# Nine groups of up to seven pairs a tile for fourteen of four, and turned blocks in the sums' banks

## The chip, the cores and the metric

The kernel runs on one core of a Trainium2 chip. The metric is the device time of one execution, in microseconds. Of the kernel before there are three runs, with a median of 2292.99 us (2291.53 to 2293.34), and one profiled execution.

## The reference

A graph with N = 12,500 nodes of H = 64 features and E = 400,000 edges; `src` and `dst` are drawn at random and sorted by `dst`. After a layer norm and a ReLU, two rounds of message passing with a GRU cell follow, and the input is added at the end:

```python
    for t in range(num_rounds):
        src = x[row]
        dest = x[col]
        m_input = jnp.concatenate([dest, src, edge_attr], axis=1)
        messages = m_input @ msg_W[t].T + msg_b[t]
        agg = jax.ops.segment_sum(messages, row, num_segments=x.shape[0])
        x = _gru_cell(agg, x, gru_Wih[t], gru_bih[t], gru_Whh[t], gru_bhh[t])
    return x
  ...
  h = jnp.maximum(_layernorm(x, axis=-1), 0.0)
  x = x + _L0_gnn_ref(h, edge_index, edge_weight1, ...)
```

Here `row` is `src` and `col` is `dst`. The message weights are linear, so the kernel sums the features of the `dest` nodes of each node's edges first, and the weights come in afterwards, in the gates. Each round is therefore a gather of 400,000 rows by `dst` and a sum of them by `src`.

## The kernel before, in words

The nodes are cut into 98 tiles of 128 for the sums (by `src`) and into windows for the rows that are gathered (by `dst`), C = 104 of them, each of at most 128 nodes. A sort at the start, up to about 741 us, puts the edges into slots: each pair of a tile and a window has 64 slots. Then come round 1 (about 741 to 1510 us) and round 2 (about 1533 to 2272 us), in which every tile goes through the same steps. Two windows make a pair: a tile has 52 pairs.

- **gather** (PE, L1298). A one-hot matrix for each window, made by DVE from the slots' lanes (`dst1`, named `planes` in the rows), times the window's rows: 2 matmuls of 128 columns for a pair, into a bank of PSUM (`ps_rows`).
- **take** (ACT, L1399). It copies the gathered rows of one unit, a group of pairs, from PSUM to SBUF as fp16.
- **scatter** (PE, L1320 in round 1, L1318 in round 2, whose operands are exchanged). The taken rows times a second one-hot matrix (`src1`, `src` in the rows): 2 matmuls for a pair, which add up in the tile's bank `ps_sum`. There are two such banks, for even and odd tiles.
- **sums** (ACT, L1410 and L1406): copies the sum of a finished tile. **node_sums** (DVE, L1525 to L1535 and L1516, L1520) makes `joined`, `scaled` and, in round 1, `extras` from it.
- **turn** (PE, L1337 to L1340; two matmuls in round 2, L1332 and L1333): transposes these blocks in `ps_T`, a bank of its own; **take_turned** (ACT, L1417) copies them out.
- **gates** (PE, L1353 and L1355), then for each pair of tiles sigmoid `rz` (ACT, L1429, odd tiles), **tanh_inputs** (DVE, L1543, L1545), tanh `cand` (ACT, L1446, even tiles), **mix** (DVE). In round 1 ACT and DVE cut the new features into two fp16 parts: high (ACT, L1435, odd tiles), the rest (**left_over**, DVE, L1561), low (ACT, L1440, even tiles).

The order on every engine is written out by hand in a function `body(s, b, half)`, called for each tile s (b is 0 for even tiles, 1 for odd ones). `in_pairs` (L62) unrolls the first few tiles and puts the others into a hardware loop of two tiles. The 52 pairs are cut into NU = 14 units, ten of 4 pairs and four of 3 (`UJ`, `PAIR_AT`). On PE, unit u of a tile is gathered and then unit u - LAG is scattered, with LAG = 3; the last three units of a tile are scattered beside the first gathers of the next. Where the small steps stand among the units is told by five numbers, `TURN_AT` 1, `SUM_AT` 3, `GATES_AT` 5, `SIGMOID_AT` 8, `TANH_AT` 3. Gathers use four rooms of one bank in turn, and one waits for the take of four units earlier.

The one-hots are made in NQ = 4 parts of a tile (2048, 2048, 1792 and 768 columns; L1499 by planes and L1503 by source). The lanes for a part are fetched by DMA from SP's queue and from POOL's (L675). In round 1 POOL also copies the edge attributes of each part into the rows (`put_attr`, L1165), and the scatter of the part's first unit waits for that. In round 2 the rows are kept in a ring of four units.

Of the kernel before, what the change touches and what calls it, by code (L numbers as in the profile page):

```python
# [22 lines left out]
P = 128  # L23
# [107 lines left out]
def build(nc, x, src, dst, attr, msg_W, msg_b, Wih, bih, Whh, bhh, out):  # L131
# [15 lines left out]
    NU = 2 * -(-J // (2 * UJ))  # L147
    UQ = -(-NU // NQ)
    FULL = J - NU * (UJ - 1)
    PAIR_AT = [u * UJ - max(u - FULL, 0) for u in range(NU + 1)]  # L150
    QUARTER_AT = [PAIR_AT[min(q * UQ, NU)] for q in range(NQ + 1)]
    assert ROUNDS > 1 and P >= C >= NT and C > HELD and 0 < LAST <= EW and (P - C) * EW <= E and E % P == 0 and PAIR_AT[NU] == J and 0 <= FULL <= NU and all(at % 2 == 0 for at in QUARTER_AT) and NU % 2 == 0 and N * P < 1 << 22 and H == 64 and NT % 2 == 0 and NU > (NQ - 1) * UQ and UQ >= LAG and N >= P
# [18 lines left out]
    SUM_AT, TURN_AT, GATES_AT, SIGMOID_AT, TANH_AT = 3, 1, 5, 8, 3  # L171
# [13 lines left out]
    with ExitStack() as ctx:  # L185
# [914 lines left out]
        def sums_round(r, scope):  # L1100
# [23 lines left out]
            ps_rows = [ps(f"ps_rows{b}", [P, 512], scope=scope) for b in range(4)]  # L1124
# [6 lines left out]
            ps_T = ps("ps_T2", [P, 512], scope=scope)  # L1131
# [47 lines left out]
            with nc.Block() as block:  # L1179
# [108 lines left out]
                def _(te):  # L1288
                    def gather(s, u, b):
# [3 lines left out]
                        wait(te, rows_ready, s * NU + u - 3)  # L1293
                        for k, j in enumerate(pairs_of(u)):
                            for half in range(2):
                                c = 2 * j + half
                                if c < C:
                                    last = nc.tensor.matmul(  # L1298
                                        ps_rows[(u + NU * b) % 4][half * SLOTS:(half + 1) * SLOTS, k * 2 * H:(k + 1) * 2 * H],
                                        dst1[q][:, (c - 2 * QUARTER_AT[q]) * SLOTS:(c - 2 * QUARTER_AT[q] + 1) * SLOTS], rows_of[r % 2][:, c, :],  # L1300
                                        start=True, stop=True)
                        last.then_inc(gathered, 1)

                    def scatter(s, u, b):
# [6 lines left out]
                        if u == 0:  # L1311
                            wait(te, joined_ready if flipped else sum_ready, s - 1)
                        for k, j in enumerate(pairs_of(u)):
                            hot = src1[q][:, (j - QUARTER_AT[q]) // 2, :, j % 2]
                            row = rows_of_unit(u, b)[:, k, :]
# [8 lines left out]
                    def turn(k, b):  # L1324
# [5 lines left out]
                        if flipped:  # L1330
                            te.wait_ge(extras_kept, 1)
                            nc.tensor.matmul(ps_T[high, 0:P], copied[b][:], ident[:], start=True, stop=True)  # L1332
                            nc.tensor.matmul(ps_T[low, 0:P], scaled[b][:], ident[:], start=True, stop=True).then_inc(turned, 1)  # L1333
# [3 lines left out]
                        nc.tensor.matmul(ps_T[low, 0:P], joined[b][:], ident[:], start=True, stop=True)  # L1337
                        nc.tensor.matmul(ps_T[high, 0:P], copied[b][:], ident[:], start=True, stop=True)
                        nc.tensor.matmul(ps_T[high, P:2 * P], extras[b][:], ident[:], start=True, stop=True)
                        nc.tensor.matmul(ps_T[low, P:2 * P], scaled[b][:], ident[:], start=True, stop=True).then_inc(turned, 1)  # L1340
# [21 lines left out]
                    def turn_extras():  # L1362
                        for v in range(2):
                            last = nc.tensor.transpose(ps_T[0:NT, v * P:(v + 1) * P], edge_sums[:, :, v], ident[:])  # L1364
                        last.then_inc(extras_turned, 1)

                    def body(s, b, half):
                        later_tile = past(s, 1)
                        for u in range(NU):
                            gather(s, u, b)  # L1370
# [6 lines left out]
                            if past(s, 2) and u == TURN_AT:  # L1377
                                turn(s - 2, b)
# [501 lines left out]
```

## Time and profile before

| | |
|---|---|
| median of three runs | 2292.99 us (2291.53 to 2293.34) |
| the profiled execution | 2290.76 us |
| its span | 2288.8 us |
| PE, PEld busy | 1507.7 (66%), 1405.6 (61%) |
| DVE, ACT busy | 2132.3 (93%), 1894.5 (83%) |
| POOL busy | 743.5 (32%) |
| takes (L1399) | 2744, 1362.3 us, mean 612 ns |
| one-hots by source (L1503) | 784, 801.4 us, mean 1022 ns |
| one-hots by planes (L1499) | 784, 515.8 us, mean 658 ns |
| scatter L1320, L1318 | 10192 each, 555.9 and 542.0 us |
| gather L1298 | 10192 a round, 545.8 and 535.4 us |
| fetch of lanes to its landing | 3.7 to 4.6 us |

The shares are over the whole span, and a third of it is the sort, where PE hardly works. For the rounds they are to be read by stage. Busy times of successive instructions overlap at their tails: from the start of one to the start of the next is less than what one lasts. PEld is the load of a matmul's weights, which runs beside the matmuls before it.

### The profile page before, as it was taken

How to read it: one execution, taken by the hardware profiler on the slowest of the kernel's cores; microseconds unless marked ns; L12 is line 12 of the kernel's file. 1: busy time of each engine (PE TensorE's matmuls, PEld its weight loads, DVE VectorE, ACT ScalarE, POOL GpSimd, SP SyncE). 2: the span in 40 equal slices, each digit the busy share in tenths (PEclk: the TensorE clock that was granted, in tenths of full speed). 3: DMA queues.
4: the chain of work that ended last, by engine and by line, in shares of the span. 5: the costliest groups of instructions: out<-in, count | busy, mean ns of one | idle time of the engine just before them, and what ended most of it. 6: DMA issues, size and time to landing. Idle time of an engine off the chain costs nothing. (4 is left out here: it accounts for less than half of the span.)

```text
span 2288.8 us, 121076 instructions
## 1 busy us (share of the span) xinstructions
PE 1507.7 (66%) x43734; PEld 1405.6 (61%) x43734; DVE 2132.3 (93%) x3394; ACT 1894.5 (83%) x4474; POOL 743.5 (32%) x1245
## 2 busy tenths in 40 slices
PE   0000000000024899999999999958999999999996
PEld 0000000000013899999999999858999999999996
DVE  8999999999967899999999999958999999999996
ACT  4778795664124899999999999958999999999996
POOL 1000000000085666666666666621222222122222
PEclk9999999999999999999999999979999999999998
DMA  6100001210233676666667777636767777777773
GB/s 124 34 0 0 0 0 36 47 23 22 56 91 88 210 228 231 221 233 228 228 233 226 229 229 229 217 124 215 244 240 240 240 240 240 239 241 239 240 241 118
DMA packets 165648, 375.64 MB, mean 164 GB/s; under 512 B 70877, under 2 KB 87427, under 8 KB 165023
## 3 DMA queue, kind: packets, MB, share of 16 engines
q1 hardware_dynamic: 114427, 191.07, 26.9%
q0 software_dynamic: 49456, 181.94, 24.0%
q10 hardware_dynamic: 1708, 1.97, 0.3%
q8 instruction: 24, 0.39, 0.1%
q14 instruction: 33, 0.27, 0.0%
HBM read 358.39 MB, written 16.17 MB: 164 GB/s over the span
## 5 line engine op out<-in xcount | busy, mean ns | idle before, releaser
L1399 ACT ACTIVATE rows<-ps_rows 128x512 f16<-128x512 f32 (+1 forms) x2744 | 1362.3, 612 | 53.3 <-PE ps_rows L1298 42.9
L1503 DVE TENSOR_TENSOR src<-iota_units,src_lane 128x2048 f16<-128x2048 f16 (+2 forms) x784 | 801.4, 1022 | 26.6 <-PE ps_sum L1318 19.2
L1320 PE MATMUL ps_sum<-rows,src 128*64 128x132 f16 x10192 | 555.9, 222 | 9.0 <-issue 1.6
L1298 PE MATMUL ps_rows<-rows_next,planes 128*64 128x128 f16 x10192 | 535.4, 219 | 36.4 <-DVE planes L1499 21.3
L1298 PE MATMUL ps_rows<-rows_now,planes 128*64 128x128 f16 x10192 | 545.8, 219 | 19.7 <-ACT rows L1399 9.2
L1318 PE MATMUL ps_sum<-src,rows 128*64 128x128 f16 x10192 | 542.0, 220 | 4.8 <-ACT rows L1399 1.2
L1499 DVE TENSOR_SCALAR planes<-planes,lane_no 128x2048 f16<-128x2048 f16 (+2 forms) x784 | 515.8, 658 | 8.7 <-DMA planes<-lanes_dram 8.6
L816 PE MATMUL ps_src<-ident,late 104*64 104x104 f32 x98 | 19.9, 380 | 642.0 <-DVE late L1051 623.4
L1298 PEld LDWEIGHTS ps_rows<-rows_now,planes 128*64 128x64 f16 x10192 | 412.2, 110 | 41.1 <-ACT rows L1399 17.9
L1298 PEld LDWEIGHTS ps_rows<-rows_next,planes 128*64 128x64 f16 x10192 | 397.8, 109 | 60.6 <-DVE planes L1499 21.9
L816 PEld LDWEIGHTS ps_src<-ident,late 104*64 104x64 f32 x98 | 13.7, 162 | 648.1 <-DVE late L1051 624.0
L1320 PEld LDWEIGHTS ps_sum<-rows,src 128*64 128x64 f16 x10192 | 396.6, 110 | 18.1 <-ACT rows L1399 16.3
L1318 PEld LDWEIGHTS ps_sum<-src,rows 128*64 128x64 f16 x10192 | 386.2, 109 | 12.9 <-ACT rows L1399 12.5
L675 POOL DMA_DIRECT2D planes<-lanes_dram x392 | 226.5, 578 | 288.1 <-DVE planes L1499 273.7
L1223 POOL COPY copied<-h 128x64 f32 (+1 forms) x196 | 66.5, 340 | 522.0 <-PE ps_T L1333 512.9
L793 POOL DMA_INDIRECT taken<-lower_dram,start_i x22 | 44.9, 2040 | 581.1 <-issue 581.1
L1165 POOL COPY rows<-attr_room 128x32 f16 (+5 forms) x392 | 220.4, 562 | 0.8 <-PE ps_sum L1320 0.4
L324 ACT ACTIVATE taken<-taken 128x3847 bf16<-128x3847 int32 x49 | 171.0, 3490 | 14.6 <-issue 14.5
L1353 PE MATMUL ps_gates<-w_first,turned_now 128*64 128x256 f32 x784 | 122.1, 378 | 3.1 <-ACT turned_now L1417 1.7
L1355 PE MATMUL ps_gates<-w_second,turned_now 128*64 128x256 f32 x784 | 122.5, 379 | 1.1 <-issue 1.1
L1355 PEld LDWEIGHTS ps_gates<-w_second,turned_now 128*64 128x64 f32 x784 | 64.8, 137 | 19.9
L1417 ACT ACTIVATE turned_now<-ps_T 128x256 f32<-128x256 f32 (+1 forms) x196 | 70.7, 361 | 3.4 <-PE ps_T L1340 2.6
(213 smaller groups left out, 2200.3 us busy)
## 6 DMA issues: line engine op xcount, KB each, us to landing
planes<-lanes_dram POOLq DMA_DIRECT2D x196, 512.0 KB, 4.4
planes<-lanes_dram SPq DMA_DIRECT2D x194, 512.0 KB, 4.6
planes<-lanes_dram POOLq DMA_DIRECT2D x98, 448.0 KB, 4.6
planes<-lanes_dram SPq DMA_DIRECT2D x97, 448.0 KB, 4.6
planes<-lanes_dram POOLq DMA_DIRECT2D x98, 192.0 KB, 3.7
planes<-lanes_dram SPq DMA_DIRECT2D x97, 192.0 KB, 3.9
rows_now<-parts_dram SPq DMA_DIRECT2D x104, 32.0 KB, 1.7
rows_next<-parts_dram SPq DMA_DIRECT2D x104, 32.0 KB, 3.5
```

What stands on the lines that cost most here:

```text
L324: nc.scalar.activation(beyond[:], src_i[:], ACT.Sign, bias=below[:, m:m + 1], accum_out=balance[:, m:m + 1]).then_inc(counts_ready, 1)
L675: plain(engine.dma_start(lanes[q], lanes_dram[bass.ds(s, 1), slots_of_quarter(q)] .broadcast_to([P, n_slots(q)]))).then_inc(lanes_in_of[r] ...
L1165: plain(nc.gpsimd.tensor_copy(rows[:, at, 2 * H:2 * H + 2], attr_two[:, bass.ds(s, 1), at, :] .rearrange("p o j v -> p (o j) v"))).then_in ...
L1298: last = nc.tensor.matmul(ps_rows[(u + NU * b) % 4][half * SLOTS:(half + 1) * SLOTS, k * 2 * H:(k + 1) * 2 * H], dst1[q][:, (c - 2 * QUART ...
L1318: last = nc.tensor.matmul(ps_sum[b][at, 0:P], row[:, at], hot, start=(j == 0), stop=(j == J - 1))
L1320: last = nc.tensor.matmul(ps_sum[b][at, 0:width], hot[:, at], row, start=(j == 0), stop=(j == J - 1))
L1353: nc.tensor.matmul(ps_gates[at, to], turned_now[b][:, at], w_first[:, r, :], start=True, stop=False)
L1355: last = nc.tensor.matmul(ps_gates[at, to], turned_now[b][:, P + at.start:P + at.stop], w_second[:, r, :], start=False, stop=True)
L1399: nc.scalar.activation(rows_of_unit(u, b)[:, :, 0:2 * H], cut(ps_rows[(u + NU * b) % 4][:])[:, 0:n, :], ACT.Copy).then_inc(rows_ready, 1)
L1417: nc.scalar.activation(turned_now[b][:, 0:n], ps_T[:, 0:n], ACT.Copy).then_inc(T_ready, 1)
L1499: nc.vector.tensor_scalar(dst1[q], lanes[q], lane_no[:, 0:1], None, ALU.is_equal).then_inc(dst1_ready, 1)
L1503: nc.vector.tensor_tensor(src1[q][:], iota_units[:].rearrange("p (o l) k -> p o l k", o=1) .broadcast_to([P, pairs_now, P, 2]), src_lane[: ...
```

## The change

The unit is no longer of a fixed size. A tile has three parts, each with units of (7, 7, 4), (7, 7, 4) and (6, 6, 4) pairs: nine units. `ps_rows` has three rooms, of two, two and one bank (8, 8 and 4 pairs), and a gather waits for the take of three units earlier. That is five banks where there were four. The fifth is the one that `ps_T` had: the turned blocks now stand in the second half of the sums' banks, columns 256 to 511 of `ps_sum[b]`. The first scatter of a tile has to wait until ACT has copied the turned blocks of the tile two before (`T_ready`), where it waited for the sums or `joined`; in round 2 the turn waits for `joined_ready` as well. LAG is 2, and the one-hots come in three parts of 2304, 2304 and 2048 columns, with three fetches of lanes and three attribute copies a tile. In round 2 the rows have the whole room of 52 pairs and no ring. The small steps stand at units 0 (turn), 2 (sums), 3 (gates), 5 (sigmoid) and 2 (tanh). No matmul is added or taken away.

```diff
-UJ = 4
-NQ = 4
+UNITS = ((7, 7, 4), (7, 7, 4), (6, 6, 4))
+UNIT_ROOM = (8, 8, 4)
+NQ = 3
...
-LAG = 3
+LAG = 2
...
-    SUM_AT, TURN_AT, GATES_AT, SIGMOID_AT, TANH_AT = 3, 1, 5, 8, 3
+    SUM_AT, TURN_AT, GATES_AT, SIGMOID_AT, TANH_AT = 2, 0, 3, 5, 2
...
-            ring = NU if r == 0 else 4
-            rows = sb("rows", [P, J if r == 0 else ring * UJ, width], F16, scope=scope)
+            rows = sb("rows", [P, J, width], F16, scope=scope)
...
-            ps_rows = [ps(f"ps_rows{b}", [P, 512], scope=scope) for b in range(4)]
+            ps_rows = [ps(f"ps_rows{b}", [P, n * P], scope=scope) for b, n in enumerate(UNIT_ROOM)]
...
-            ps_T = ps("ps_T2", [P, 512], scope=scope)
+            ps_T = [bank[:, 2 * P:4 * P] for bank in ps_sum]
...
-                        wait(te, rows_ready, s * NU + u - 3)
+                        wait(te, rows_ready, s * NU + u - UQ + 1)
...
                         if u == 0:
-                            wait(te, joined_ready if flipped else sum_ready, s - 1)
+                            wait(te, T_ready, s - 1)
+                            if flipped and not past(s, 2):
+                                te.wait_ge(extras_kept, 1)
...
                         if flipped:
-                            te.wait_ge(extras_kept, 1)
+                            te.wait_ge(joined_ready, bank + k - b + 1)
...
                             if flipped and not later_tile and u == TURN_AT:
                                 turn_extras()
+                            if past(s, 2) and u == TURN_AT:
+                                turn(s - 2, b, b)
                             if u >= LAG:
                                 scatter(s, u - LAG, b)
                             elif later_tile:
                                 scatter(s - 1, NU - LAG + u, 1 - b)
-                            if past(s, 2) and u == TURN_AT:
-                                turn(s - 2, b)
...
-                            take(s, u, b)
+                            take(s, u)
...
+                            if past(s, 2) and u == TURN_AT:
+                                take_turned(s - 2, b, b)
                             if one_back and u == SUM_AT:
                                 take_sum(s - 1, 1 - b)
-                            if past(s, 2) and u == TURN_AT + 1:
-                                take_turned(s - 2, b)
...
                         one_hots(s, 2)
                         if more and b == 0 and past(s, 6):
                             left_over(half - 3)
-                        one_hots(s, 3)
```

PE in round 1, the start of a tile up to its gates, before. L1337 to L1340 are the turn, L1298 gathers, L1320 scatters.

```order
L1337 MATMUL ps_T<-ident,joined 64x128
L1338 MATMUL ps_T<-ident,copied 64x128
L1339 MATMUL ps_T<-ident,extras 64x128
L1340 MATMUL ps_T<-ident,scaled 64x128
L1298 MATMUL ps_rows<-rows_now,planes 64x128 x8
L1320 MATMUL ps_sum<-rows,src 64x132 x6
L1298 MATMUL ps_rows<-rows_now,planes 64x128 x8
L1320 MATMUL ps_sum<-rows,src 64x132 x8
L1298 MATMUL ps_rows<-rows_now,planes 64x128 x8
L1320 MATMUL ps_sum<-rows,src 64x132 x8
L1298 MATMUL ps_rows<-rows_now,planes 64x128 x8
L1320 MATMUL ps_sum<-rows,src 64x132 x8
L1353 MATMUL ps_gates<-w_first,turned_now 64x256 x2
L1355 MATMUL ps_gates<-w_second,turned_now 64x256 x2
```

The same place after the change, with one row more ahead of it, the tile's first gather (L1294 gathers, L1335 to L1338 turn, L1318 scatters):

```order
L1294 MATMUL ps_rows<-rows_now,planes 64x128 x14
L1335 MATMUL ps_sum<-ident,joined 64x128
L1336 MATMUL ps_sum<-ident,copied 64x128
L1337 MATMUL ps_sum<-ident,extras 64x128
L1338 MATMUL ps_sum<-ident,scaled 64x128
L1318 MATMUL ps_sum<-rows,src 64x132 x12
L1294 MATMUL ps_rows<-rows_now,planes 64x128 x14
L1318 MATMUL ps_sum<-rows,src 64x132 x8
L1294 MATMUL ps_rows<-rows_now,planes 64x128 x8
L1318 MATMUL ps_sum<-rows,src 64x132 x14
L1294 MATMUL ps_rows<-rows_now,planes 64x128 x14
L1318 MATMUL ps_sum<-rows,src 64x132 x14
```

The turn has moved up behind the first gather, ahead of the previous tile's last two scatters. The first scatter of the new tile is the one of 14 behind the third gather; it comes two units behind its gather, where it came three.

ACT in an odd tile of round 1, from the middle of the tile to its end, before. L1399 is the take, with its pairs as the second number of the shape, L1435 high, L1429 the sigmoid.

```order
L1399 ACTIVATE rows<-ps_rows 128x4x128 x4
L1435 ACTIVATE new_parts<-h 128x2x64
L1399 ACTIVATE rows<-ps_rows 128x4x128
L1429 ACTIVATE rz<-ps_gates 128x256
L1399 ACTIVATE rows<-ps_rows 128x4x128
L1399 ACTIVATE rows<-ps_rows 128x3x128 x4
```

After, where the take is L1397, high L1433 and the sigmoid L1427:

```order
L1397 ACTIVATE rows<-ps_rows 128x7x128 x2
L1433 ACTIVATE new_parts<-h 128x2x64
L1397 ACTIVATE rows<-ps_rows 128x4x128
L1427 ACTIVATE rz<-ps_gates 128x256
L1397 ACTIVATE rows<-ps_rows 128x6x128 x2
L1397 ACTIVATE rows<-ps_rows 128x4x128
```

Two takes of 7 pairs stand in the place of four of 4 ahead of high, and the take behind the sigmoid has 6 pairs. That take of 6 is the one that the seventh scatter of an odd tile waits for.

## Rows read from the trace of the kernel before

**Rows 1.** Windows: busy us (instructions) of each engine in both rounds

```profile
900.00:1500.00 600.00, 585.78 (x17277) 551.93 (x17271) 577.77 (x1238) 577.43 (x1390) 386.89 (x734) 1.00 0.69 228
1700.00:2250.00 550.00, 539.23 (x16405) 508.06 (x16401) 534.47 (x933) 545.36 (x1269) 118.52 (x187) 1.00 0.72 240
```

**Rows 2.** Timeline of L1429, ACT's sigmoid, in round 1

```profile
L1429 ACT ACTIVATE rz<-ps_gates x5: 395/398/398, 1194.2 to 1256.1; 128x256 f32<-128x256 f32 x5
```

**Rows 3.** Timeline of L1429, round 2

```profile
L1429 ACT ACTIVATE rz<-ps_gates x5: 427/427/427, 1881.5 to 1940.5; 128x256 f32<-128x256 f32 x5
```

**Rows 4.** Timeline of PE, an odd tile of round 2: start, us

```profile
1908.09 0.61 PE L1353 MATMUL ps_gates<-w_first,turned_now 128*64 128x256 f32 x4
...
1908.95 0.40 PE L1298 MATMUL ps_rows<-rows_next,planes 128*64 128x128 f16 x8
...
1910.77 0.35 PE L1298 MATMUL ps_rows<-rows_next,planes 128*64 128x128 f16 x6
...
1911.56 0.35 PE L1298 MATMUL ps_rows<-rows_next,planes 128*64 128x128 f16 x6
1912.00 0.42 PE L1318 MATMUL ps_sum<-src,rows 128*64 128x128 f16 x8
```

**Rows 5.** Timeline of PE, round 1: odd tile, then the even one

```profile
1210.12 0.36 PE L1298 MATMUL ps_rows<-rows_now,planes 128*64 128x128 f16 x6
1210.61 0.43 PE L1320 MATMUL ps_sum<-rows,src 128*64 128x132 f16 x8
...
1211.03 0.34 PE L1320 MATMUL ps_sum<-rows,src 128*64 128x132 f16 x6
1211.57 0.41 PE L1298 MATMUL ps_rows<-rows_now,planes 128*64 128x128 f16 x8 [0.19 <-ACT rows L1399]
...
1213.04 0.42 PE L1298 MATMUL ps_rows<-rows_now,planes 128*64 128x128 f16 x8
```

**Rows 6.** Timeline of ACT, the same tiles

```profile
1208.99 0.31 ACT L1435 ACTIVATE new_parts<-h 128x128 f16 x1
1209.19 0.60 ACT L1399 ACTIVATE rows<-ps_rows 128x512 f16<-128x512 f32 x1
1209.67 0.40 ACT L1429 ACTIVATE rz<-ps_gates 128x256 f32<-128x256 f32 x1
1209.93 3.25 ACT L1399 ACTIVATE rows<-ps_rows 128x512 f16<-128x512 f32 x7
...
1213.58 0.60 ACT L1399 ACTIVATE rows<-ps_rows 128x512 f16<-128x512 f32 x1 [0.40 <-PE ps_rows L1298]
1214.08 0.38 ACT L1417 ACTIVATE turned_now<-ps_T 128x256 f32<-128x256 f32 x1
1214.34 0.60 ACT L1399 ACTIVATE rows<-ps_rows 128x512 f16<-128x512 f32 x1
```

**Rows 7.** Waits, round 1: engine line <- releaser: us, times, longest

```profile
PEld ps_sum L1320 <- ACT rows L1399: 12.0, 43, 0.3
```

**Rows 8.** Timeline of DVE, the same tiles

```profile
1207.94 0.56 DVE L1503 TENSOR_TENSOR src<-iota_units,src_lane 128x768 f16<-128x768 f16 x1
1208.42 0.74 DVE L1499 TENSOR_SCALAR planes<-planes,lane_no 128x2048 f16<-128x2048 f16 x1
1209.09 1.21 DVE L1503 TENSOR_TENSOR src<-iota_units,src_lane 128x2048 f16<-128x2048 f16 x1
1210.22 0.25 DVE L1525 SCALAR_TENSOR_TENSOR joined<-sums 128x64 f32<-128x64 f32 x1
...
1215.24 0.41 DVE L1499 TENSOR_SCALAR planes<-planes,lane_no 128x768 f16<-128x768 f16 x1
1215.56 0.56 DVE L1503 TENSOR_TENSOR src<-iota_units,src_lane 128x768 f16<-128x768 f16 x1
```

**Rows 9.** Timeline of DVE and POOL, where the copy is late

```profile
1111.12 1.22 DVE L1503 TENSOR_TENSOR src<-iota_units,src_lane 128x2048 f16<-128x2048 f16 x1
...
1111.32 1.09 POOL L1165 COPY rows<-attr_room 128x32 f16 x1
```

More of the change, by code:

```diff
@@ L146, in build @@
     J = -(-C // 2)
[L147 to L150, printed above, removed]
+    SIZES = [n for part in UNITS for n in part]
+    NU, UQ = len(SIZES), len(UNIT_ROOM)
+    PAIR_AT = list(itertools.accumulate(SIZES, initial=0))
     QUARTER_AT = [PAIR_AT[min(q * UQ, NU)] for q in range(NQ + 1)]
-    assert ROUNDS > 1 and P >= C >= NT and C > HELD and 0 < LAST <= EW and (P - C) * EW <= E and E % P == 0 and PAIR_AT[NU] == J and 0 <= FULL <= NU and all(at % 2 == 0 for at in QUARTER_AT) and NU % 2 == 0 and N * P < 1 << 22 and H == 64 and NT % 2 == 0 and NU > (NQ - 1) * UQ and UQ >= LAG and N >= P
+    assert ROUNDS > 1 and P >= C >= NT and C > HELD and 0 < LAST <= EW and (P - C) * EW <= E and E % P == 0 and PAIR_AT[NU] == J and all(n <= most for part in UNITS for n, most in zip(part, UNIT_ROOM)) and all(at % 2 == 0 for at in QUARTER_AT) and N * P < 1 << 22 and H == 64 and NT % 2 == 0 and NU == NQ * UQ and UQ >= LAG and N >= P
     HA = H + 2
@@ L1288, in _, with gather @@
                 def _(te):
-                    def gather(s, u, b):
+                    def gather(s, u):
                         q = u // UQ
@@ L1322, in scatter, with turn @@
                         last.then_inc(scattered, 1)
-                    def turn(k, b):
+                    def turn(k, b, bank):
                         te.wait_ge(copied_ready, k + 1)
@@ L1330, in turn @@
                         if flipped:
-                            te.wait_ge(extras_kept, 1)
-                            nc.tensor.matmul(ps_T[high, 0:P], copied[b][:], ident[:], start=True, stop=True)
-                            nc.tensor.matmul(ps_T[low, 0:P], scaled[b][:], ident[:], start=True, stop=True).then_inc(turned, 1)
+                            te.wait_ge(joined_ready, bank + k - b + 1)
+                            nc.tensor.matmul(ps_T[bank][high, 0:P], copied[b][:], ident[:], start=True, stop=True)
+                            nc.tensor.matmul(ps_T[bank][low, 0:P], scaled[b][:], ident[:], start=True, stop=True).then_inc(turned, 1)
                             return
@@ L1336, in turn @@
                         te.wait_ge(joined_ready, k + 1)
[L1337 to L1340, printed above, removed]
+                        nc.tensor.matmul(ps_T[bank][low, 0:P], joined[b][:], ident[:], start=True, stop=True)
+                        nc.tensor.matmul(ps_T[bank][high, 0:P], copied[b][:], ident[:], start=True, stop=True)
+                        nc.tensor.matmul(ps_T[bank][high, P:2 * P], extras[b][:], ident[:], start=True, stop=True)
+                        nc.tensor.matmul(ps_T[bank][low, P:2 * P], scaled[b][:], ident[:], start=True, stop=True).then_inc(turned, 1)
                     def gates(k, b, half):
```

39 lines of the change are left out of this document (19 added, 20 removed).

## The prediction

> **What bounds the kernel now.** I read the busy time by stage first. Both rounds run at the full granted clock, and three engines are nearly full at once: in round 1 PE 98%, DVE 96%, ACT 96%; in round 2 PE 98%, DVE 97%, ACT 99% [rows 1]. So the time is two stretches of 49 pairs of tiles, plus a sort that the edit leaves alone. ACT's sigmoid runs once a pair: five of them lie 61.9 us apart in round 1 (15.48 a pair) and 59.0 in round 2 (14.75) [rows 2, 3]. Over the whole of round 1 a pair is a little longer: 17,277 matmul records at 224 a tile are 77.1 tiles in 600 us, 15.56 a pair [rows 1].
>
> What orders the three full engines comes from the timelines. PE issues a gather of 8 and a scatter of 8 in (1910.77 - 1908.95)/4 = 0.455 us, and the gates, 1908.09 to 1908.95, in 0.86 [rows 4]. Per pair that is 208 x 0.0569 = 11.83, gates 1.72, turned blocks 4 matmuls at a gate's time halved with its columns (0.11) = 0.44: 13.99 of PE's own in round 2. In 14.75 it waits 0.76. In round 1 the turn has four matmuls, not two (+0.44), and the scatter 132 columns (+0.06): 14.49 of 15.48, 0.99 waited. The two large waits are seen. In the odd tile the scatter after a gather of 6 could begin at 1210.12 + 0.17 and begins at 1210.61, 0.32 late [rows 5]; ACT has high, a take and the sigmoid before the take it needs, which starts at 1209.93 and lasts 0.60 or more [rows 6]. In round 2 that wait is 1912.00 - 1911.73 = 0.27 [rows 4]. At the loop's branch a scatter of 6 from 1211.03 is issued by 1211.21 and the next gather starts at 1211.57: 0.36 [rows 5]. So PE is the bound, with a chain through ACT once a pair; the waits' own list puts 12.0 us in 600 on this scatter [rows 7].
>
> **The edit, part by part.**
>
> ACT: 9 takes a tile for 14. A take of 512 columns is followed by the next instruction after 0.48 us (1209.19 to 1209.67), the turned copy of 256 columns after 0.26 (1214.08 to 1214.34) [rows 6]: 0.86 ns a column and 0.04 fixed. Five fixed parts are 0.2 us a tile less of ACT. PE is not behind ACT's sum but behind single takes, so I put nothing of it on the path; what remains is that a take is longer: 0.81 for 7 pairs, 0.70 for 6, and 0.12 more to its end (0.60 lasts against 0.48). [...]
>
> Odd tile, the chain from the gates' end: gather of 14, 0.39; its end to the take 0.32 (eight from 1213.04, take at 1213.58 [rows 5, 6]); take of 7 pairs 0.81; high 0.20 (1208.99 to 1209.19); take of 4, 0.48; sigmoid 0.26; take of 6 to its end 0.82; 0.05 to the scatter. Sum 3.33 in round 1, 3.13 in round 2 without high. PE's own up to that scatter is 98 matmuls, 2.79. It waits 0.54 and 0.34, where it waited 0.32 and 0.27.
>
> Even tile: a scatter lags two units, not three. Gather 0.39 + 0.32 + take 0.93 + 0.05 = 1.69, against 1.59 that PE has (56 matmuls from the start of that gather): 0.10 a pair, new in both rounds.
>
> Loop: the gather behind the branch followed the end of the last take by 0.63 (that take ended some 0.09 before the scatter at 1211.03). If it is counted from there, a scatter of 12 (0.35) covers more, and 0.63 - 0.05 - 0.35 = 0.23 is left. If the branch costs 0.36 behind any scatter, that is the other end, +0.13 a pair, +13 us over both rounds. I take 0.23.
>
> Turned blocks in the sums' banks: the first scatter of a tile now waits until ACT has copied them. Gather of 14 (0.39), 0.32, take to 1.52, turned copy 0.38, 0.05 to the scatter: 1.95 in round 1, while PE has three gathers, the turn and two scatters, 56 matmuls and 0.44, together 2.03. That is no wait by 0.08, and since two chains so close slip now and then, I take 0.05 a tile. In round 2 the copy has half the columns (0.35, an estimate from the 0.38), so 1.92, but PE's turn is 0.22 shorter, 1.81: 0.11, taken as 0.13 with the same slips. No row of before has this wait; its ends are 0 and 0.38 (a whole turned copy [rows 6]), and I stay near the first because both sides of the race are counted from rows.
>
> DVE: 6 one-hots a tile for 8. The matrix by planes takes 0.67 for 2048 columns and 0.32 for 768, the source one-hot 1.13 and 0.48 [rows 8]: fixed parts of 0.11 and 0.09, so 0.20 less a tile. PE rarely waits for DVE, so its price is 0, apart from one thing. In round 1 POOL copies the edge attributes into the rows; such a copy (started 1111.32, 1.09 us) ends when DVE's one-hot (1111.12, 1.22) ends [rows 9], and now and then PE's scatter waits for it. That is the 0.08 between a quiet pair and the mean. With fewer and rarer meetings I take most of it as gone: -0.06. [...]
>
> Moved at no cost: turn_extras and the higher bank of its output, once; the whole room of rows in round 2 (ACT then needs no scatter to free a unit, and no wait on one is among the large ones above); the fetches of lanes in three parts, whose bytes stay the same.
>
> Sum. Round 1: after the edit 0.54 + 0.23 + 0.10 + 2 x 0.05 = 0.97 waited a pair against 0.99, -1 over 49 pairs, and -3 from the disturbances: -4, to which I add +1 for the drain with wide units. Round 2: 0.34 + 0.23 + 0.10 + 0.26 = 0.93 against 0.76, +0.17, +8 us; its start -1, its drain +1. Together +5 on the profiled run's 2290.8: 2296. The median of the three runs is 2.2 above the profiled one, so the forecast is 2298.
>
> **Rivals.**
>
> No change: the first scatter finds its bank free. If the turned copy is in time in both rounds, 0.10 and 0.26 a pair go, 18 us, and if the branch costs its 0.36 again, 13 come back: 2293. For it: PE's own work is not changed by a single matmul, and it fills 98% [rows 1]. Against: two new waits, each on a count that is late already.
>
> Slower by more: the first scatter's wait. From the point where the take of 896 columns and the turned copy end later than the 1.9 us that PE has, every tile pays. At 0.2 us a tile in both rounds (twice what I take, half a copy) the sum grows by (0.15 + 0.07) x 98 = 21: 2319; at 0.1, with the branch at 0.36 in part, 2307. For it: ACT is 96 to 99% busy, and any slip before the take is handed on to PE in the same tile, since the lag is one unit shorter. Against: ACT has 0.2 us a tile more air.
>
> Faster through DVE and POOL: in round 1 DVE does not rest (its idle is the gap inside its own sums), so PE's pace could be DVE's. Then round 1 takes -0.20 x 98 = -20, and with +8 in round 2 the time is 2281. For it: 96% busy [rows 1]. Against: PE's waits are named after ACT, not after DVE.
>
> Faster through ACT's load: ACT is at 99% in round 2. If that is a bound and not a crowd behind PE, 0.2 x 98 in round 2 goes as well: 2293 - 40 = 2253 in full, 2273 for half. [...]
>
> **How the numbers follow.** What a measurement of this kernel can tell from no change is 0.2%, 4.6 us: 2288.4 to 2297.6. The forecast has 0.42 (own range 2293 to 2304; 0.12 of it within the bound, 0.30 above), no change 0.18, slower by more 0.20, faster through DVE 0.12, through ACT 0.08. So faster 0.20, same 0.12 + 0.18 = 0.30, slower 0.30 + 0.20 = 0.50. The range 2283 to 2312 leaves out the lower part of DVE's and all of ACT's case (0.11), and the upper half of slower by more (0.09); above, it takes in the branch's other end.
>
> **What the profile after would show.** Nine takes a tile, and six one-hots; ACT's share down by 2 to 3 points in both rounds, DVE's as much. Idle of PE before the scatter of unit 0 on the turned copy (0.05 and 0.13 a tile): if it is none, round 2 is no slower. Idle before the scatter of unit 6 in odd tiles, 0.54 and 0.34. Pairs 15.5 us apart in round 1 and 14.92 in round 2. I am wrong if round 1's pair falls to 15.1 (DVE was the bound), if round 2's falls below 14.7, or if the wait behind the branch is still 0.36.

## The result, and the profile after

The changed kernel takes 2307.68 us (median of five runs, 2301.03 to 2307.91), the kernel before in the same comparison 2291.53 (2289.23 to 2293.34): a ratio of 1.0061 with a 95% interval of 1.0048 to 1.0074. It is 16 us slower; 5 were forecast. The profiled execution took 2307.91 us, its span is 2306.3.

The windows of both rounds after, as [rows 1]:

```profile
900.00:1500.00 600.00, 585.11 (x17124) 537.99 (x17118) 559.19 (x1073) 555.60 (x994) 297.84 (x575) 1.00 0.67 226
1700.00:2250.00 550.00, 543.37 (x16149) 506.43 (x16149) 520.04 (x772) 522.25 (x880) 122.80 (x185) 1.00 0.69 236
```

ACT's busy time fell by 3.6 points in round 1 (577.43 to 555.60) and by 4.2 in round 2, DVE's by 3.1 and 2.6: the edit does what it says on both engines. PE's busy share stays, but in the 600 us of round 1 it has 17,124 matmuls where it had 17,277. What two engines gave up, PE did not get. How far apart the pairs are shows L1427, the sigmoid, as in [rows 2, 3]; round 1, then round 2:

```profile
L1427 ACT ACTIVATE rz<-ps_gates x6: 385/387/388, 1247.4 to 1325.7; 128x256 f32<-128x256 f32 x6
```

```profile
L1427 ACT ACTIVATE rz<-ps_gates x5: 390/391/397, 1892.8 to 1952.8; 128x256 f32<-128x256 f32 x5
```

78.3/5 = 15.66 us a pair, and 60.0/4 = 15.00. Before it was 15.48 and 14.75. These are quiet pairs, in stretches where the sigmoids are evenly spaced; over 900 to 1500 us the mean is 15.70 (15.56 before). The first gather to the last is 7.7 us longer in round 1 and 9.2 in round 2. The waits of round 1 (us in total, times, longest):

```profile
ACT rows L1397 <- PE ps_rows L1294: 40.0, 117, 0.6
...
PEld ps_sum L1318 <- ACT rows L1397: 17.1, 39, 0.8
...
PE ps_sum L1318 <- ACT rows L1397: 10.1, 38, 0.3
```

ACT now waits 40.0 us for gathers, where it was 17.0; the scatter's weight load waits 17.1 us for takes with up to 0.8 each, where [rows 7] has 12.0 and 0.3. The timeline of PE shows where. First the end of an even tile and the start of the odd one behind it, which have no branch between them, then the end of the odd tile and the loop's branch at its end (start us, us):

```profile
1303.32 0.52 PE L1318 MATMUL ps_sum<-rows,src 128*64 128x132 f16 x12
1303.67 0.55 PE L1294 MATMUL ps_rows<-rows_now,planes 128*64 128x128 f16 x14
1304.06 0.28 PE L1336 MATMUL ps_sum<-ident,copied 128*64 128x128 f32 x1
...
1309.06 0.50 PE L1294 MATMUL ps_rows<-rows_now,planes 128*64 128x128 f16 x12
1309.53 0.60 PE L1318 MATMUL ps_sum<-rows,src 128*64 128x132 f16 x14
1309.97 0.50 PE L1294 MATMUL ps_rows<-rows_now,planes 128*64 128x128 f16 x12
1310.30 0.40 PE L1318 MATMUL ps_sum<-rows,src 128*64 128x132 f16 x8
1310.54 0.39 PE L1294 MATMUL ps_rows<-rows_now,planes 128*64 128x128 f16 x8
1311.19 0.54 PE L1318 MATMUL ps_sum<-rows,src 128*64 128x132 f16 x12 [0.27 <-ACT rows L1397]
1311.83 0.58 PE L1294 MATMUL ps_rows<-rows_now,planes 128*64 128x128 f16 x14
1312.33 0.29 PE L1335 MATMUL ps_sum<-ident,joined 128*64 128x128 f32 x1
```

A gather matmul takes 0.0276 us and a scatter 0.0295, from start to start (1303.32 to 1306.50 without the turn's 0.44: 1.38 for 50 gathers and 1.36 for 46 scatters). So in the odd tile the gather at 1309.06 is issued by 1309.39 and the next scatter starts at 1309.53, 0.14 late; the gather at 1310.54 ends at 1310.76 and the scatter of unit 6 comes at 1311.19, 0.43 late; that scatter is issued by 1311.54 and the next tile's gather starts at 1311.83, 0.29 late; and the turn behind it comes at 1312.33, 0.11 late (0.08 in round 2). At the even tile's end the same row of work has no gap at all (1303.32 + 0.35 = 1303.67; + 0.39 = 1304.06). ACT in the odd tile:

```profile
1308.56 0.92 ACT L1397 ACTIVATE rows<-ps_rows 128x896 f16<-128x896 f32 x1 [0.64 <-PE ps_rows L1294]
1309.37 0.30 ACT L1433 ACTIVATE new_parts<-h 128x128 f16 x1
1309.57 0.59 ACT L1397 ACTIVATE rows<-ps_rows 128x512 f16<-128x512 f32 x1
1310.05 0.39 ACT L1427 ACTIVATE rz<-ps_gates 128x256 f32<-128x256 f32 x1
1310.32 2.01 ACT L1397 ACTIVATE rows<-ps_rows 128x768 f16<-128x768 f32 x3
```

The take of 7 pairs starts at 1308.56, and high (L1433) and the sigmoid (L1427) lie between it and the take of 6 pairs at 1310.32, which PE's scatter at 1311.19 waited for. The takes themselves have the length that was worked out: 0.81 us from one start to the next (1308.56 to 1309.37), and by shape

```profile
L1397 ACT ACTIVATE rows<-ps_rows 128x896 f16<-128x896 f32 x305 | 281.0, 921 | 44.7 <-PE ps_rows L1294 40.0
L1397 ACT ACTIVATE rows<-ps_rows 128x512 f16<-128x512 f32 x229 | 136.8, 598 | 0.0
L1397 ACT ACTIVATE rows<-ps_rows 128x768 f16<-128x768 f32 x154 | 118.2, 821 | 0.0
```

In round 2 the first scatter of an even tile, which now waits for the turned copy, is only 0.03 late (1896.32 + 0.22 = 1896.54, start at 1896.57); in odd tiles it is 0.11:

```profile
1896.32 0.41 PE L1294 MATMUL ps_rows<-rows_next,planes 128*64 128x128 f16 x8
1896.57 0.60 PE L1316 MATMUL ps_sum<-src,rows 128*64 128x128 f16 x14
```

### The profile page after: what moved, and what is told of

Its sections match the earlier page's. It is cut to its first block and busy times, and to the rows that moved or that the text cites. A ratio compares the mean times of both kernels' runs of the same rounds, so it can differ in the third digit from the quotient of the medians.

```text
span 2306.3 us, 114718 instructions
## 1 busy us (share of the span) xinstructions
PE 1529.2 (66%) x43734; PEld 1403.7 (61%) x43734; DVE 2106.6 (91%) x3002; ACT 1852.8 (80%) x3494; POOL 639.6 (28%) x1049
## 5 line engine op out<-in xcount | busy, mean ns | idle before, releaser
L1397 ACT ACTIVATE rows<-ps_rows 128x896 f16<-128x896 f32 (+2 forms) x1764 | 1292.6, 792 | 113.6 <-PE ps_rows L1294 99.4
L1501 DVE TENSOR_TENSOR src<-iota_units,src_lane 128x2304 f16<-128x2304 f16 (+1 forms) x588 | 778.8, 1324 | 58.3 <-PE ps_sum L1316 37.1
L1497 DVE TENSOR_SCALAR planes<-planes,lane_no 128x2304 f16<-128x2304 f16 (+1 forms) x588 | 472.3, 803 | 20.0 <-DMA planes<-lanes_dram 16.9
L1318 PE MATMUL ps_sum<-rows,src 128*64 128x132 f16 x10192 | 458.4, 222 | 18.8 <-ACT rows L1397 13.9
L1316 PE MATMUL ps_sum<-src,rows 128*64 128x128 f16 x10192 | 460.4, 221 | 8.0 <-issue 3.0
L1294 PE MATMUL ps_rows<-rows_next,planes 128*64 128x128 f16 x10192 | 445.0, 219 | 27.6 <-DVE planes L1497 20.3
L1294 PE MATMUL ps_rows<-rows_now,planes 128*64 128x128 f16 x10192 | 438.6, 219 | 13.7 <-DVE planes L1497 7.4
L1294 PEld LDWEIGHTS ps_rows<-rows_next,planes 128*64 128x64 f16 x10192 | 355.8, 110 | 49.6 <-DVE planes L1497 20.9
L1294 PEld LDWEIGHTS ps_rows<-rows_now,planes 128*64 128x64 f16 x10192 | 348.3, 110 | 39.0 <-issue 20.0
L1318 PEld LDWEIGHTS ps_sum<-rows,src 128*64 128x64 f16 x10192 | 348.7, 110 | 36.0 <-ACT rows L1397 22.7
L675 POOL DMA_DIRECT2D planes<-lanes_dram x294 | 156.6, 533 | 344.9 <-DVE planes L1497 316.8
L1164 POOL COPY rows<-attr_room 128x36 f16 (+3 forms) x294 | 143.3, 487 | 4.7 <-PE ps_sum L1318 4.7
L1415 ACT ACTIVATE turned_now<-ps_sum 128x256 f32<-128x256 f32 (+1 forms) x196 | 63.9, 326 | 3.4 <-PE ps_sum L1338 2.6
```

Of the source, the lines that this page charges most:

```text
L675: plain(engine.dma_start(lanes[q], lanes_dram[bass.ds(s, 1), slots_of_quarter(q)] .broadcast_to([P, n_slots(q)]))).then_inc(lanes_in_of[r] ...
L1164: plain(nc.gpsimd.tensor_copy(rows[:, at, 2 * H:2 * H + 2], attr_two[:, bass.ds(s, 1), at, :] .rearrange("p o j v -> p (o j) v"))).then_in ...
L1294: last = nc.tensor.matmul(ps_rows[u % UQ][half * SLOTS:(half + 1) * SLOTS, k * 2 * H:(k + 1) * 2 * H], dst1[q][:, (c - 2 * QUARTER_AT[q]) ...
L1316: last = nc.tensor.matmul(ps_sum[b][at, 0:P], row[:, at], hot, start=(j == 0), stop=(j == J - 1))
L1318: last = nc.tensor.matmul(ps_sum[b][at, 0:width], hot[:, at], row, start=(j == 0), stop=(j == J - 1))
L1397: nc.scalar.activation(rows_of_unit(u)[:, :, 0:2 * H], cut(ps_rows[u % UQ][:])[:, 0:n, :], ACT.Copy).then_inc(rows_ready, 1)
```

## The experiments

Each is against the kernel before on the same chip. "The changed kernel" is the one of the diff. Differences between two experiments are of their medians, and the chips are not the same; by the ratios, the 57 and 30 us that experiments 1 and 7 gain on the changed kernel are 51 and 25.

**1. LAG 3 with the wide units.**

```diff
-LAG = 2
+LAG = 3
-    SUM_AT, TURN_AT, GATES_AT, SIGMOID_AT, TANH_AT = 2, 0, 3, 5, 2
+    SUM_AT, TURN_AT, GATES_AT, SIGMOID_AT, TANH_AT = 3, 0, 3, 5, 2
...
-                        if flipped:
+                        if flipped and u < NU - LAG + 2:
```

The last two lines are the end of round 2, where a third unit is left to scatter but only two tiles to turn.

> The changed kernel with LAG 3 in place of 2 (the sums are taken at unit 3 with it). Theory A, the wait behind long takes: a scatter that waited for its take has that take a unit earlier, so the waits of 0.06 before the fourth and 0.44 before the sixth scatter go to the gathers' waits on their rooms, which are shorter by a scatter of 14 (0.41 us); a pair falls by 0.2 to 0.4 us in both rounds, 10 to 20 us a round, and the time is 2275 to 2295. Theory B, the turned blocks in the sums' banks: the copy now has a unit more, 0.07 a tile goes in round 2 alone, 7 us, and round 1 stays at 15.66 a pair: 2300. Theory C, ACT's chain is what it is wherever the scatter stands, since the room is only given back by the take: no change, 2305 to 2310.

Measured: 2250.86 us, a ratio of 0.984 (0.9824 to 0.9856). That is 57 us less than the changed kernel, and 39 less than before. No theory gave as much. The pairs, round 1 and round 2:

```profile
L1427 ACT ACTIVATE rz<-ps_gates x6: 384/386/386, 1250.8 to 1327.6; 128x256 f32<-128x256 f32 x6
```

```profile
L1427 ACT ACTIVATE rz<-ps_gates x6: 394/394/394, 1884.9 to 1955.8; 128x256 f32<-128x256 f32 x6
```

15.36 and 14.18: most of it is in round 2, which comes down to 0.2 of PE's own 13.99. Theory A is right about the place: the takes are no shorter, and in round 2 no gather or scatter waits for them. In round 1 one gather a pair still does, the one behind the branch, for 0.21 us. In round 2 the gap behind the branch is gone without any change to the loop (an odd tile's last scatter, the next tile's first gather, and the scatter behind its turn):

```profile
1900.06 0.43 PE L1316 MATMUL ps_sum<-src,rows 128*64 128x128 f16 x8
1900.30 0.58 PE L1294 MATMUL ps_rows<-rows_next,planes 128*64 128x128 f16 x14
...
1901.05 0.55 PE L1316 MATMUL ps_sum<-src,rows 128*64 128x128 f16 x12
```

1900.06 + 0.24 = 1900.30: the gather follows at once. Its 0.39 and the turn's 0.22 end at 1900.91, so 0.14 of the former 0.37 is left. In round 1 another wait stands before the turn, on DVE's `extras`:

```profile
PEld ps_sum L1335 <- issue: 21.8, 75, 1.0
...
PE ps_sum L1335 <- DVE extras L1533: 10.2, 40, 0.9
```

**2. LAG 2 in the kernel before.**

```diff
-LAG = 3
+LAG = 2
```

> The kernel before with LAG 2 alone. Theory A: with takes of 4 pairs a shorter lag costs on the same places as in the changed kernel: before the scatters behind high, the sigmoid and tanh. Each of them has 0.45 us less cover, so a pair grows by 0.2 to 0.6 us and the time by 20 to 60 us (2310 to 2350): then the lag is what the wide units pay back, and not the width. Theory B and C: the time stays within 5 us of the kernel before (2287 to 2297).

Measured: 2416.44 us, 1.0555 (1.0542 to 1.0569), 127 us slower, twice the upper end. With units of 4 pairs PE has three gathers and two scatters, 1.13 us, from the start of a gather to its own scatter, and the way through a plain take is 0.22 + 0.32 + 0.60 + 0.05 = 1.19. So a scatter behind a plain take is up to 0.06 late, and one whose take stands behind another step of ACT 0.25 to 0.34: in round 1 behind high and the sigmoid in odd tiles, and behind the turned copy in every tile. The list has 40.0 us of waits for takes in 600, 141 times. The changed kernel has the same lag and is 16 us slower, not 127: the wide units, with the other parts of the edit, pay most of it back.

**3. Three parts of one-hots alone.**

```diff
-NQ = 4
+NQ = 3
-                        one_hots(s, 3)
```

> The kernel before with its one-hots in three parts (2560, 2560 and 1536 columns) and nothing else. DVE has 0.20 us a tile less. If DVE or its meeting with POOL's copies has a share in the period: round 1 falls by 0.05 to 0.2 a tile, 5 to 20 us (2272 to 2287). If PE's waits for ACT are all there is: within 4 us of before, or some us slower where DVE gives a part later (2288 to 2298).

Measured: 2281.70 us, 0.9966 (0.9954 to 0.9978): 8 us faster, near the small end of the first case. A quiet pair of round 1 stays at 15.48; the gain is in fewer disturbed pairs there (a mean of 15.46 for 15.56 over 900 to 1500 us). In round 2 a quiet pair is 0.08 shorter, but from the first gather to the last the round takes 732.3 us for 732.9.

**4. Turned blocks in the sums' banks alone**, with the turn at unit 0:

```diff
-    SUM_AT, TURN_AT, GATES_AT, SIGMOID_AT, TANH_AT = 3, 1, 5, 8, 3
+    SUM_AT, TURN_AT, GATES_AT, SIGMOID_AT, TANH_AT = 3, 0, 5, 8, 3
-            ps_T = ps("ps_T2", [P, 512], scope=scope)
+            ps_T = [bank[:, 2 * P:4 * P] for bank in ps_sum]
...
-                            wait(te, joined_ready if flipped else sum_ready, s - 1)
+                            wait(te, T_ready, s - 1)
...
```

The order of the turn and its copy within a unit is that of the changed kernel.

> The kernel before with the turned blocks in the sums' banks and the turn at unit 0, and nothing else; a bank stands free. Theory B, sharing is the cost: a tile's first scatter waits for the turned copy, 0.07 us a tile or more in round 2, and for joined before the turn; 7 to 15 us slower (2298 to 2307). Theory A: with takes of 4 pairs the copy is in time by 0.4 us, so it is within 4 us of before, or faster by the turn's wait in even tiles of round 1 (0.1 us a pair, 5 us): 2285 to 2294.

Measured: 2292.20 us, 1.0013 (1.0004 to 1.0022): 3 us slower, inside what theory A allows.

**5. Both alone, together.** The diffs of 3 and 4.

> The kernel before with both parts of the edit that were tried alone, three parts of one-hots and turned blocks in the sums' banks, still 14 units and LAG 3. If they add up, -7.8 and +2.7: 2284 (2280 to 2288), and what the changed kernel with LAG 3 has beyond that, 33 us, is the wide units' own. If they don't add: under 2275 or over 2292.

Measured: 2298.79 us, 1.0045 (1.0031 to 1.0059). They do not add: 2284 was the sum, 15 us less. A larger first part of the one-hots (2560 columns) stands ahead of the node sums on DVE, and the turn at unit 0 needs these sums at once. PE in round 1:

```profile
1296.85 0.42 PE L1298 MATMUL ps_rows<-rows_now,planes 128*64 128x128 f16 x8
1297.25 0.29 PE L1339 MATMUL ps_sum<-ident,joined 128*64 128x128 f32 x1
```

The gather is issued by 1297.07 and the turn comes at 1297.25, 0.18 late. At the same place, a tile's start without a branch, the turn follows at once in a quiet pair of experiment 4 (first part 2048 columns) and of the changed kernel (2304). The expectation had a rule for what is left to the wide units, and that rule can't be used.

**6. LAG 3 and the turn at unit 1.** Experiment 1, with

```diff
-    SUM_AT, TURN_AT, GATES_AT, SIGMOID_AT, TANH_AT = 3, 0, 3, 5, 2
+    SUM_AT, TURN_AT, GATES_AT, SIGMOID_AT, TANH_AT = 3, 1, 3, 5, 2
```

> The changed kernel with LAG 3 (sums at unit 3), and the turn and its copy at unit 1 for unit 0. In the first of these, round 1 still has 0.2 to 0.5 us before the turn on DVE's extras (10.2 us named in 600 us, 21.8 with no name). Theory A, these waits are PE's: they go, a pair of round 1 falls from 15.39 to 14.7 to 15.1, 14 to 30 us in all, round 2 stays: 2221 to 2237. Theory D, DVE's own round trip of 15.1 us a pair is now the bound of round 1, and the wait moves to the one-hots: 0 to 10 us, 2240 to 2251.

Measured: 2279.34 us, 0.9953 (0.9939 to 0.9967): 28 us slower than experiment 1, and neither theory had it. Round 1 gained 0.06 to 0.09 a pair; round 2 lost 0.54:

```profile
L1427 ACT ACTIVATE rz<-ps_gates x6: 392/392/392, 1884.7 to 1958.3; 128x256 f32<-128x256 f32 x6
```

```profile
PE ps_sum L1316 <- ACT turned_now L1415: 9.0, 34, 0.3
```

The wait is named for round 2; PE stands 0.45 us before the first scatter of an even tile and 0.20 in odd ones. This is the rival "slower by more" of the prediction, at another setting: when the turned copy stands behind the second take of 7 pairs, the first scatter of each tile, whose wait on `T_ready` stands ahead of it in the kernel, comes late (9.0 us in 34 waits). At unit 0 the same wait is 0 to 0.11.

**7. Sigmoid and high later, LAG 2.** The changed kernel, with

```diff
-    SUM_AT, TURN_AT, GATES_AT, SIGMOID_AT, TANH_AT = 2, 0, 3, 5, 2
+    SUM_AT, TURN_AT, GATES_AT, SIGMOID_AT, TANH_AT = 2, 0, 3, 7, 2
```

> The changed kernel with LAG 2 as it is; in odd tiles high stands behind take 6 and the sigmoid behind take 7, not behind takes 4 and 5. Theory A, chain of takes in the odd tile: take 6 comes 0.46 us earlier in round 1 and 0.26 in round 2, the wait of 0.44 (0.25) before the scatter of unit 6 goes, and some of it comes back before scatter 7 or the next tile's first gather: a pair falls by 0.1 to 0.4 in round 1 and 0 to 0.2 in round 2, 5 to 25 us: 2282 to 2302. Rival: the same chain ends one unit later and behind the loop's branch, where nothing covers it: no change or some us slower, 2305 to 2315.

Measured: 2277.90 us, 0.9952 (0.9939 to 0.9966), 30 us less than the changed kernel; theory A, some 4 us beyond its range. Round 1:

```profile
L1427 ACT ACTIVATE rz<-ps_gates x6: 407/408/409, 1249.7 to 1325.8; 128x256 f32<-128x256 f32 x6
```

```profile
PEld ps_sum L1318 <- ACT rows L1397: 2.1, 3, 1.2
```

15.22 for 15.66; the wait of 17.1 us on this scatter is 2.1. Round 2 has 14.74 for 15.00. The scatter in front of the branch no longer stands idle, and still the gather behind the branch comes 0.26 late in both rounds; the part on the prediction takes this up.

**8. LAG 3, node sums first.** Experiment 1, and on DVE

```diff
-                        one_hots(s, 0)
                         if past(s, 2):
                             node_sums(s - 2, b)
+                        one_hots(s, 0)
```

> The changed kernel with LAG 3, and DVE makes a tile's node sums ahead of the first one-hot, not behind it: joined and extras come some 2 us earlier and every one-hot part 0 comes 0.8 us later. Theory A: the turn's wait in round 1 goes as with the turn at unit 1, 14 to 30 us in round 1: 2221 to 2237. Theory D, DVE is the bound there: 2240 to 2255, PE waits for the one-hots instead.

Measured: 2243.54 us, 0.9796 (0.9782 to 0.9809): theory D's range, 7 us less than experiment 1.

**9. All three, the fastest version.** Experiment 8 with the sigmoid at unit 7.

> The changed kernel with the three edits that helped alone: LAG 3, node sums ahead of the first one-hot, sigmoid at unit 7 (high at 6). In its forerunner with the sigmoid at 5, round 1 has 0.24 us (two tiles' mean 0.13) before the gather that needs take 4's room, and a pair of 15.09; round 2 is at 14.19 of PE's own 13.98. Theory A, takes behind high and the sigmoid: round 1 falls to 14.7 to 14.95 a pair, 7 to 19 us, round 2 by 0 to 5 us: 2220 to 2237. Theory D, DVE holds round 1 at 15.0 to 15.1: 2238 to 2245.

Measured: 2241.61 us (2234.43 to 2244.38), 0.978 (0.9765 to 0.9794). It is experiment 8 within noise, theory D. DVE in round 1, one pair:

```profile
1281.72 0.29 DVE L1559 TENSOR_TENSOR new_rest<-h,new_parts 128x128 f32<-128x128 f16 x1
...
1282.52 0.26 DVE L1531 TENSOR_SCALAR scaled<-h,edge_sums 128x64 f32 x1 [0.15 <-DVE edge_sums L1529]
...
1290.25 0.25 DVE L1531 TENSOR_SCALAR scaled<-h,edge_sums 128x64 f32 x1 [0.15 <-DVE edge_sums L1529]
...
1296.87 0.30 DVE L1559 TENSOR_TENSOR new_rest<-h,new_parts 128x128 f32<-128x128 f16 x1
```

From one `new_rest` to the next are 15.15 us, and in them the timeline names no idle of DVE but the 0.15 behind its own edge sums, twice; the other gaps between its instructions are 0.11 or less. The pair is 15.1 in this round: DVE is the bound there, and PE (14.18 a pair) in round 2.

**10. The sigmoid later in the kernel before.**

```diff
-    SUM_AT, TURN_AT, GATES_AT, SIGMOID_AT, TANH_AT = 3, 1, 5, 8, 3
+    SUM_AT, TURN_AT, GATES_AT, SIGMOID_AT, TANH_AT = 3, 1, 5, 12, 3
```

> The kernel before with the sigmoid at unit 12 for 8 (high at 11). It has the same wait on a take behind them, 0.32 and 0.27 us a pair. Theory A, it is their place that costs, as with the changed kernel: 5 to 25 us faster (2265 to 2285). Rival: with rooms of 4 pairs the wait only moves to the units behind, 11 to 13, and to the first gather behind the branch: within 4 us of before, or slower up to 2300.

Measured: 2279.96 us, 0.9961 (0.9948 to 0.9974), 9 us faster. Round 1 and round 2:

```profile
L1429 ACT ACTIVATE rz<-ps_gates x5: 441/441/443, 1254.1 to 1316.2; 128x256 f32<-128x256 f32 x5
```

```profile
L1429 ACT ACTIVATE rz<-ps_gates x6: 477/478/478, 1887.3 to 1960.0; 128x256 f32<-128x256 f32 x6
```

Round 2 has 14.54 for 14.75: theory A. Round 1 stays at 15.5, although the wait is gone there too. That is DVE's own time with four parts, 0.38 more than the 15.15 of experiment 9: apart from the 0.15 in its sums DVE is listed with 2.7 us idle in 600. PE now stands 0.29 before the first scatter of odd tiles, which comes 0.32 behind DVE's source one-hot and 0.25 behind POOL's copy beside it; which of the two it waits for is not separated. So in the kernel before, round 1 stood on two bounds at once, PE's waits (15.48) and DVE.

**11. Node sums first, LAG 2.** The changed kernel with the diff of experiment 8.

> The changed kernel as it is, LAG 2, with DVE's node sums ahead of the first one-hot. The turn at unit 0 in even tiles waits 0.08 to 0.09 us behind the branch. If DVE's late joined and extras are its cause, that goes: 4 us a round, 2297 to 2303 with the first one-hot late at no cost. If the wait is POOL's copy or the branch's own, no change: 2304 to 2308.

Measured: 2304.53 us, 1.0060 (1.0045 to 1.0075): no change against the changed kernel's 1.0061. The turn in even tiles is 0.13 late where it was 0.11 (0.08 in round 2), so that is not DVE's.

**12. A loop of four tiles on PE.** The changed kernel, with

```diff
-                    in_pairs(te, NT, body, PEEL["te"])
+                    for i in range(6):
+                        body(i, i % 2, i // 2)
+                    with te.Fori(1, (NT - 6) // 4 + 1) as i:
+                        for k in range(4):
+                            body(4 * i + 2 + k, k % 2, 2 * i + 1 + k // 2)
```

> The changed kernel with LAG 2 as it is; only PE's own loop has four tiles in its body for two (six tiles ahead of it, not four), so every second pair has no branch between its tiles. The gap behind the scatter of unit 6 of odd tiles (0.29 us a pair in both rounds) is the open one. If the branch is its cost, it goes in every second pair: -0.15 a pair on average, 14 us, 2291 to 2296, and in the trace pairs alternate. If it is the wait for the last takes, which only stands there: no change, 2303 to 2308. In between, if DVE or ACT take over what PE gives back: 2296 to 2303.

Measured: 2724.14 us, 1.1876 (1.1843 to 1.1909). Neither case nor the one between foresaw this. The time was lost to something else (the last section), but the trace answers the question. An odd tile's end in the middle of the loop's body:

```profile
1247.34 0.39 PE L1294 MATMUL ps_rows<-rows_now,planes 128*64 128x128 f16 x8
1247.99 0.55 PE L1318 MATMUL ps_sum<-rows,src 128*64 128x132 f16 x12 [0.26 <-ACT rows L1401]
1248.37 0.55 PE L1294 MATMUL ps_rows<-rows_now,planes 128*64 128x128 f16 x14
1248.76 0.28 PE L1335 MATMUL ps_sum<-ident,joined 128*64 128x128 f32 x1
```

The scatter of unit 6 is as late as ever (1247.34 + 0.22 = 1247.56, start at 1247.99), but 1247.99 + 0.35 = 1248.34 and the gather starts at 1248.37, and the turn at 1248.76 without a wait. All 14 such ends between 900 and 1500 us have the scatter 0.43 late; in 6 of them the gather follows within 0.03, in the others 0.08 to 0.82 behind, in a trace full of the gaps of the last section. The 0.29 and the 0.1 are the branch's.

## Why the prediction was right in sign and short in size

The direction held, and so did its reason: new and longer waits on PE outweigh what ACT and DVE save. The size was a third of the measured one. The time lies above the likeliest case's own range (2293 to 2304), where "slower by more" was priced, and it is not that rival's mechanism that put it there. The waits of PE in a quiet pair, by the prediction's terms:

| term, us a pair | round 1: forecast | measured | round 2: forecast | measured |
|---|---|---|---|---|
| odd tile, takes behind high and sigmoid | 0.54 | 0.60 | 0.34 | 0.36 |
| loop's branch, with the turn behind it | 0.23 | 0.39 | 0.23 | 0.37 |
| even tile, with small gaps | 0.10 | 0.16 | 0.10 | 0.17 |
| first scatter on the turned copy | 0.10 | 0 | 0.26 | 0.13 |
| sum | 0.97 | 1.15 | 0.93 | 1.03 |

- **The bound.** "PE is the bound, with a chain through ACT once a pair" holds for the changed kernel: two edits that shorten or cover this chain alone, experiments 1 and 7, gave 57 and 30 us. It was incomplete for round 1 of the kernel before: DVE's own time was 15.5 there as well (experiment 10). The rival that named DVE had the bound right and its gain wrong: 0.2 us a tile less of DVE is worth nothing in a quiet pair until PE's waits are gone too, and then it is what lets round 1 fall from 15.5 to 15.1 (experiments 9 and 10). The rival of ACT's load had no part: ACT's busy time fell by 4.2 points in round 2, and the round grew by 9.2 us.
- **The term that was furthest off is the branch.** The sum counted the gap from the end of the last take, 0.63, less 0.05 and less the scatter of 12, 0.35, and took 0.23; it named 0.36 as the other end, "+13 us over both rounds". The way of counting was right and two amounts were not. From the take's end to the gather are 0.69 and not 0.63 (medians; 0.64 before), so the gap is 0.69 - 0.05 - 0.35 = 0.29. And the turn, which now stands behind this gather, is 0.11 late in round 1 and 0.08 in round 2, for which the sum has no term. Together 0.15 a pair more than forecast, 15 us, where the whole sum was short by 11. That the total is near the other end is a coincidence: a branch with a fixed gap of 0.36 behind any scatter is not what the traces show.
- **What hides the branch.** Under `PEldq` the trace lists steps of L77, the line of the loop (L76 in the kernel before). First the changed kernel, round 1, the branch between 1311.19 and 1311.83, then experiment 1, the one between 1900.06 and 1900.30:

```profile
L77 PEldq ALU_OP  x1: 32/32/32, 1311.3 to 1311.3; - x1
```

```profile
L77 PEldq ALU_OP  x1: 32/32/32, 1899.7 to 1899.7; - x1
```

From this first step of the branch to the next gather is 0.57 to 0.58 us (medians) in the kernel before, the changed kernel and experiment 7, in both rounds, and in round 2 of experiment 1. What differs is when it starts. Where the take before the last scatter has only just ended, it starts 0.11 behind that take's end (the changed kernel and experiment 7), or 0.06 (the kernel before); in experiment 1 the last scatter's take is long over, and the step starts 0.34 ahead of the scatter. So the scatter's length does cover its part, as the prediction had it, and in experiment 1, where the branch's first step comes 0.34 ahead of the scatter and not 0.06 behind it as in the changed kernel, none of it is left. Experiment 7 shows that it is not enough that PE itself stands no more.
- **The chain of the odd tile** was forecast to 0.06: 3.33 from the gates to the scatter; 1307.80 to 1311.19 in the trace, 3.39.
- **The first scatter's wait** was too high in both rounds (0.05 and 0.13 a tile; 0 and 0.07), which hid 11 us of the other errors. That the forecast was no further off is owed to this in part, and is luck. The mechanism is real: experiment 6 met it at 0.20 and 0.45 us a tile.
- **Costs at nothing.** ACT's 0.2 us a tile was put at nothing; no experiment tries it by itself, and nothing in the table asks for it. DVE's was worth 8 us alone (experiment 3), in fewer disturbed pairs. They went down in the changed kernel as well (the mean of round 1 is 0.04 above a quiet pair, for 0.08), somewhat less than the 0.06 of the forecast; the rest of DVE's gain is inside the waits. The shared banks cost 3 us alone and 17 on top of the three parts (experiment 5 against 3): an interaction that the prediction did not look for, since it priced the edits one by one. In the changed kernel the order on DVE makes no difference (experiment 11).
- **What the prediction did not ask** is whether LAG had to fall. The third room allows LAG 3 (a gather waits for the take three units back in any case), and with it the same units are 39 us faster than before, not 16 slower. The 57 us are the largest gain in this study.
- **What one take costs** was counted from the rows (0.86 ns a column and 0.04 fixed): 0.81 for 896 columns from start to start, and 0.81 was measured (1308.56 to 1309.37). One lasts 0.92 for 896 columns, 0.82 for 768 and 0.60 for 512, so 0.11 of the take of 896 overlaps what follows.

Still open: why experiment 5's two parts cost 15 us more together than their sum. The turn's wait in odd tiles, some 0.2 a pair, accounts for round 1. In round 2 the turn behind the branch is 0.20 late in experiments 4 and 5 alike (14.86 and 14.90 a pair), and why the three parts then give nothing back, as they do alone (14.69 for 14.77), is not known. Open too is why the branch starts 0.11 behind the take in the changed kernel and 0.06 before.

## What to carry to other kernels

Here fewer and wider instructions saved busy time (21.8 us on ACT and 18.6 on DVE in 600 of round 1) that the pair did not gain by, and lengthened the way from a gather to the first use of its result (a take lasts 0.92 us for 0.60); count the distance in time, not in units, before shortening the lag, and try the lag by itself. Where a step such as a sigmoid sits ahead of a result that the bound engine waits for, its place counts: here moving it and high by two units gave 30 us. The loop's branch, 0.57 us from its first step to the next gather, was hidden only where PE's last wait ahead of it ended early (experiment 1: the first step 0.34 ahead of the last scatter); where it ended late, 0.29 was left. Two engines sat within 1% of the same period in round 1 of the kernel before (PE with its waits 15.48, DVE 15.5), and shortening either alone left a quiet pair where it was: 15.48 in experiment 3, 15.5 in experiment 10.

## What was not expected of the hardware

When PE's loop body is four tiles long (its weight loads and matmuls double from some 900 to some 1,800), the DMA queue that the page calls `instruction` has 434 packets for 24, and PE stands still once a turn (22 times 3.7 to 5.9 us in round 1). The queue of the page, of the changed kernel and of experiment 12 (packets, MB, share):

```profile
q8 instruction: 24, 0.39, 0.1%
```

```profile
q8 instruction: 434, 7.11, 1.1%
```

(7.11 - 0.39)/46 = 0.15 MB a turn of the loop (23 turns in each round, an estimate that gives the whole difference to them). PE at the branch:

```profile
1226.04 0.55 PE L1318 MATMUL ps_sum<-rows,src 128*64 128x132 f16 x12
1231.50 0.84 PE L1294 MATMUL ps_rows<-rows_now,planes 128*64 128x128 f16 x14 [4.91 <-issue]
```

1226.04 + 0.35 to 1231.50 is 5.1 us; two packets of this queue, 0.03 MB, start within them. What they carry, and whether PE waits for them, no row shows. There is a gap within the body as well (a turn's two pairs take some 17 and 23 us); the 417 us over the changed kernel are 9 a turn. Behind the idle the matmuls are slower too (14 in 0.84 us where it is 0.55), and the granted clock of the 12 us from 1226 on is 0.86, where it is 1.00 from 1240 to 1252. With two tiles in the body the queue has no packet between 794.2 and 1542.7 us, in which PE's loop branches 46 times; with four it has 167 there.
